# When the statistics of x1 are taken: a later place on VectorE, ScalarE and GpSimd in a two-layer graph kernel

## The chip, the cores and the metric

The kernel runs on one core of a Trainium2 chip. The metric is the device time of the whole program in microseconds: a median of 557.08 us over 3 runs (556.97 to 557.21). All data is float32 in HBM: a dense 4096 x 4096 adjacency matrix (67 MB) and node rows x of 4096 x 128.

## The reference, cut to what matters

```python
h = relu(layernorm(x))                       # first norm
x = x + gnn0(h, adj, weight, bias)           # x1: hyperbolic layer, support = adj @ x_tangent
h = relu(layernorm(x))                       # second norm: mean and variance of x1, row by row
x = x + gnn1(h, context, adj, ...)           # attention layer over the nonzeros of adj
```

Inside gnn0, after `support = adj @ x_tangent`, each row goes through expmap0, a projection, logmap0, a relu, expmap0 and a projection. All of these scale a row by a number made of its norm, so the kernel needs only sums of squares, powers, one tanh and a product. In gnn1 the logits are left[i] + right[j], and left and right are products of the 4096 x 256 context with two vectors.

## The kernel before, in words

**Phase 1** multiplies adj by x_tangent. It goes through 8 chunks c of 512 output rows. A chunk is 8 tiles of 1 MB, a tile 4 units, so a chunk has 32 units k. For each unit VectorE turns a block of adj (`turn_block`, L999) into one of four slots `turned`, TensorE multiplies it (L716, four matmuls), and ScalarE takes its signs for two units at once, a half (`signs`, L871, 16 halves a chunk), as the mask that phase 2 needs. VectorE may write unit k only when TensorE has done unit k - 4 and ScalarE has done the half with that unit. Tiles come by DMA into 6 slots, four at the end; two quarters of each are issued by SyncE, the other two by ScalarE after the odd halves (L299).

**The work behind a chunk.** The 512 rows p that chunk p has multiplied are finished while chunk p + 1 is being multiplied. Each engine has its steps at fixed places of its own loop:

- ScalarE: copy of the product after half 0, squares after half 4, tanh after half 9 of chunk p + 1; the normalised rows h2 (`normed`, L848, four activations) after half 2 of chunk p + 2.
- VectorE: relu after unit 7 (L1131), row sums after units 12 and 13 (L1135, L1139), then `spread` (L1145, bn_stats of x1) after units 28 and 29 and `variance` (L1152) after unit 30, all in chunk p + 1.
- GpSimd, in one list for p = 0 to 6: `shrink` (powers, L558 to L562), a piece of other work, `residual` (L569 to L573, which makes x1 in `xk`), `store_x1` (L589, four DMAs), a piece, `affine` (L579 to L582, scale and shift of the norm), a piece, `load_x` (L596, four DMAs that load the next x rows into `xk`).

The pieces are `beside(n)`: n even is a product of a part of context with a vector (L492), n odd the sums of such a product by halving (L501, 8 additions), for n = 0 to 15; n = 16 is `sums_and_rows` (L505 to L507), then `store_rows`, `widen_largest` and `exponents`. Pieces 0 to 7 run before p = 0, and piece 8 + 3p + j follows in p.

The waits that tie them together: `residual` waits for the tanh and for the x rows loaded; `spread` waits for `x1_ready`; `affine` waits for `var_ready`; `normed` waits for `norm2_ready` from `affine`; `load_x(p + 1)` waits for `h2_ready` from `normed`, because `normed` reads the same `xk`; `shrink(p + 1)` waits for `sums_ready`; relu(p + 1) waits for `x1_ready` of p.

**Phase 2** codes edges on VectorE and ScalarE from the mask and multiplies them by the weighted h2 rows on TensorE (L749).

Of the kernel before, what the change touches and what calls it, by code (L numbers as in the profile page):

```python
# [58 lines left out]
BESIDE_FIRST = 8  # L59
# [27 lines left out]
def bass_two_graph_layers(nc, x, adj, weight, bias, context, w_common, w_left, b_left, w_right, b_right, out):  # L87
# [3 lines left out]
    NC = N // CH  # L91
# [4 lines left out]
    with ExitStack() as ctx:  # L96
# [60 lines left out]
        def halves_of(dt, shape):  # L157

            n = L * CH
            return ([view(room, at * slot_bytes + half * n, shape, dt) for at in range(SLOTS)] for half in (0, 1))  # L160
        signs_of, _ = halves_of(I8, [L, CH])
# [279 lines left out]
        def _(pool):  # L441
# [46 lines left out]
            def product_of(w, part):  # L488

                ks = slice(part * BESIDE, (part + 1) * BESIDE)  # L490
                room_of = first_products if part == last_part else products
                side(tt(room_of, cx[:, ks, :], v_rows[:, w, :].unsqueeze(1).broadcast_to([P, BESIDE, C]), ALU.mult))  # L492

            def sum_of(w, part):

                ks = slice(part * BESIDE, (part + 1) * BESIDE)
                room_of = first_products if part == last_part else products
                n = C // 2
                while n:
                    dst = room_of[:, :, 0:n] if n > 1 else lr[:, w, ks].unsqueeze(2)  # L500
                    side(tt(dst, room_of[:, :, 0:n], room_of[:, :, n:2 * n], ALU.add))  # L501
                    n //= 2

            def sums_and_rows():
                tt(r_col[:], lr[:, 1, :], wlr[:, 3:4].broadcast_to([P, NK]), ALU.add).then_inc(r_ready, 1)  # L505
                side(tt(lr[:, 0, :], lr[:, 0, :], wlr[:, 2:3].broadcast_to([P, NK]), ALU.add))
                tt(neg_l, constants[:, 2:3].broadcast_to([P, NK]), lr[:, 0, :], ALU.subtract).then_inc(neg_ready, 1)  # L507
# [31 lines left out]
            def beside(n):  # L539

                w, part = turns[n // 2] if n < 2 * len(turns) else (None, None)
                if part is not None:
                    product_of(w, part) if n % 2 == 0 else sum_of(w, part)
                elif n == 2 * len(turns):
                    sums_and_rows()
                elif n == 2 * len(turns) + 1:
                    store_rows()
                elif n == 2 * len(turns) + 2:
                    widen_largest()
                elif n == 2 * len(turns) + 3:  # L550
                    exponents()
# [23 lines left out]
            def affine(p):  # L575

                pool.wait_ge(var_ready, p + 1)
                chain = Steps(pool, post_step, p * POOL_POST + 7)
                nc.gpsimd.tensor_scalar(post[:, 44:48], mv[:, :, 0], -1.0, None, ALU.mult)  # L579
                chain(nc.gpsimd.tensor_scalar(post[:, 40:44], mv[:, :, 1], LN_EPS, None, ALU.add))  # L580
                chain(tt(post[:, 48:52], post[:, 40:44], powers[:, 0:L], ALU.pow))
                tt(post[:, 36:40], post[:, 44:48], post[:, 48:52], ALU.mult).then_inc(norm2_ready, 1)  # L582
# [22 lines left out]
            for p in range(NC - 1):  # L605
                shrink(p)
                beside(BESIDE_FIRST + 3 * p + 0)
                if p == NC - 2:
                    scaled_weights()
                residual(p)  # L610
                store_x1(p)
                beside(BESIDE_FIRST + 3 * p + 1)
                affine(p)
                beside(BESIDE_FIRST + 3 * p + 2)
                load_x(p + 1)

            pool.wait_ge(weight_cols, 1)
# [142 lines left out]
        def _(act):  # L760
# [94 lines left out]
            def signs(c, parity):  # L855
                number = isinstance(c, int)
                acc_of[0] = acc[1 - parity]
                steps = {}
                if c >= 1:
                    copy, squares, tanh, _ = post_steps(c - 1)  # L860
                    steps = {0: copy, 4: squares, 9: tanh}
                if c >= 2:
                    steps[2] = post_steps(c - 2)[3]
                if c == NC - 2:
                    steps[7] = exponentials
                mc = mask[:, c].rearrange("p (s l) (h i) -> p l h s i", l=L, h=2)
                for half in range(TH):
                    act.wait_ge(block_turned, c * NK + HB * (half + 1))
                    slots = half % HALVES * HB
                    (l, h), s = run_and_half(c, half // HALVES), half % HALVES * L  # L870
                    nc.scalar.activation(mc[:, l, h, s:s + L],  # L871
                                         turned[:, slots:slots + HB, :].rearrange("p s (j i) -> p (s j) i", j=2),
                                         ACT.Sign, bias=constants[:, 4:5], scale=EDGE_SCALE).then_inc(
                        half_signed, 1)
                    if number and c == 0:
                        for n in range(XT_AHEAD + half * HB, min(NK, XT_AHEAD + (half + 1) * HB)):
                            bias_part(n)
                    if half in steps:
                        steps[half]()
                    if half % HALVES == HALVES - 1:  # L880
                        tile = behind[c * NC + half // HALVES]
                        if tile is not None:
                            load_tile(act, tile // NC, tile % NC, HIGH)
# [63 lines left out]
        def _(dve):  # L947
# [175 lines left out]
            def post_steps(p):  # L1123
                first = isinstance(p, int) and p == 0
                chain = Steps(dve, dve_step, p * POST + step.n)

                def relu():
                    dve.wait_ge(support_turned, p + 1)
                    if not first:
                        dve.wait_ge(x1_ready, p)  # L1130
                    v.tensor_scalar(relu_u[:], support, 0.0, None, ALU.max).then_inc(relu_ready, 1)  # L1131

                def sums_u():
                    dve.wait_ge(u_squared, p + 1)
                    v.reduce_sum(post[:, 0:4], sq1, AX_X)  # L1135

                def sums_relu():
                    dve.wait_ge(relu_squared, p + 1)
                    v.reduce_sum(post[:, 4:8], sq2, AX_X).then_inc(sums_ready, 1)  # L1139

                def spread(ls):
                    if ls[0] == 0:
                        dve.wait_ge(x1_ready, p + 1)
                    for l in ls:
                        ins = v.bn_stats(stats[:, l, :], xk[:, l, :])  # L1145
                    if ls[-1] == L - 1:
                        chain(ins)

                def variance():
                    v.memset(post[:, 61:62], 0.0)  # L1150
                    for l in range(L):
                        ins = v.bn_aggr(mv[:, l, :], stats[:, l, :])  # L1152
                    ins.then_inc(var_ready, 1)
                return {7: relu, 12: sums_u, 13: sums_relu, 28: lambda: spread((0, 1)), 29: lambda: spread((2, 3)),
                        30: variance}


            def turn(c, parity):
                number = isinstance(c, int)
                steps = {} if number and c == 0 else post_steps(c - 1)  # L1160
                for k in range(NK):
                    if not (number and c == 0 and k < TSLOTS):
                        turn_block(c, k)
                    if number and c == 0 and k // L % 2 == 0:
                        for k_ in blocks_of(c, k):
                            tangent(tangent_order.index(k_))
                    if k in steps:
                        steps[k]()
                    if c == NC // 2 and k == 15:
                        dve.wait_ge(r_ready, 1)  # L1170
                        v.reduce_max(extreme[:, 0:1], r_col[:], AX_X).then_inc(top_ready, 1)
                        dve.wait_ge(neg_ready, 1)
                        v.transpose(neg_rows, neg_l).then_inc(neg_turned, 1)
                    if c == NC // 2 + 1 and k == 3:
                        dve.wait_ge(top_spread, 1)
                        v.reduce_max(extreme[:, 1:2], ps_top, AX_X).then_inc(top_ready, 1)
            for c in range(NC):
                turn(c, c % 2)
            last = [f for _, f in sorted(post_steps(NC - 1).items())]

            def compare(c, parity, g):
                slot_free(dve, c, g)
# [140 lines left out]
```

## Time and profile before

| | us |
|---|---|
| median of 3 runs | 557.08 |
| the profiled execution, whole | 554.63 |
| its span, first to last instruction | 552.8 |
| TensorE busy in it | 480.3 |
| VectorE busy | 447.1 |
| ScalarE busy | 314.0 |
| GpSimd busy | 271.7 |

All times in the rows and in the prediction are microseconds from the start of the span of that one execution. In a timeline, a line is: start, duration, engine, source line, operation, output and input, count of merged instructions, and in brackets the idle time ahead of it with the engine that ended it. The chain of waits is the path that ended last, followed back from the end.

### The profile page before, as it was taken

Reading aid. Unit: us, or ns where it says so; the run is one execution under the profiler, and the core shown is the slowest. Engines: PE = TensorE matmul, PEld = TensorE weight load, DVE = VectorE, ACT = ScalarE, POOL = GpSimd, SP = SyncE. Lnnn points to the kernel's source line nnn. Section 1 sums busy time; section 2 is a strip of 40 time slices with the busy share of each in tenths; the row PEclk is TensorE's granted clock in tenths of the full one; section 3 lists DMA queues with packets and bytes.
Section 4 is the critical chain, followed back from the end, with each engine's and each line's share of the span. In section 5 each row is a group of like instructions: output and inputs, shape, how many; then the busy total and the mean of one; then the engine's idle time right before and its main releaser. Section 6 shows DMA issues by size and latency. Waiting matters only on the chain.

```text
span 552.8 us, 9390 instructions
## 1 busy us (share of the span) xinstructions
PE 480.3 (87%) x3209; PEld 413.2 (75%) x3209; DVE 447.1 (81%) x907; ACT 314.0 (57%) x466; POOL 271.7 (49%) x348
## 2 busy tenths in 40 slices
PE   1733879999999999999994777899999999999995
PEld 1622758877787788888883556788888888888884
DVE  3997878777787798888888899968788787878763
ACT  1584767748586778686866632535353535353521
POOL 6840899999999675535357996202020202020200
PEclk9985999999999999999997879999999999999998
DMA  7899999999999999998970000110101010101010
GB/s 171 186 234 223 252 300 301 275 280 266 311 289 320 260 332 320 338 293 218 273 194 20 22 18 28 32 40 20 39 18 41 13 46 8 52 2 38 1 39 20
DMA packets 91851, 84.75 MB, mean 153 GB/s; under 512 B 7552, under 2 KB 89728, under 8 KB 91808
## 3 DMA queue, kind: packets, MB, share of 16 engines
q1 hardware_dynamic: 56032, 48.64, 35.4%
q10 hardware_dynamic: 33424, 31.20, 20.5%
q0 software_dynamic: 2352, 4.35, 2.9%
q8 instruction: 25, 0.41, 0.3%
q14 instruction: 18, 0.15, 0.1%
HBM read 79.96 MB, written 4.21 MB: 152 GB/s over the span
## 4 chain that ended last, share of the span: by engine, by line
PE 54%; POOL 24%; DVE 7%; SPq 7%; issue 3%; DMA 3%; ACT 2%; ACTq 0%; POOLq 0%; DVEq 0%
PE ps L749 35%; PE ps L716 19%; POOL mask L501 8%; POOL mask L492 7%; SPq L382 3%; SPq L299 2%; DVE room L1234 2%; DMA mask<-in_L_gnn_context_dram 2%; DVE room L1201 2%; SPq L373 2%; DVE room L1185 1%; POOL out_dram L589 1%; POOL post L559 1%; POOL xk L596 1%; DVE room L1208 1%
## 5 line engine op out<-in xcount | busy, mean ns | idle before, releaser
L716 PE MATMUL ps<-room 128*128 128x256 f32 x1024 | 227.9, 382 | 28.5 <-DVE room L1117 22.7
L749 PE MATMUL ps<-room 128*128 128x258 f16 x2048 | 232.3, 276 | 20.5 <-POOL room L629 15.0
L749 PEld LDWEIGHTS ps<-room 128*128 128x128 fp8e4 x2048 | 200.5, 98 | 52.3 <-issue 16.0
L716 PEld LDWEIGHTS ps<-room 128*128 128x128 f32 x1024 | 193.4, 191 | 60.6 <-DVE room L999 27.5
L871 ACT ACTIVATE mask<-room,constants 128x1024 int8<-128x1024 f32 x128 | 146.1, 1145 | 59.0 <-DVE room L999 56.3
L999 DVE STREAM_TRANSPOSE room<-room 128x512 f32<-128x512 f32 x184 | 124.5, 697 | 19.8 <-PE ps L716 11.2
L643 POOL TENSOR_TENSOR h_room<-h_room 128x512 f32<-128x512 f32 x7 | 8.9, 1275 | 146.3 <-DVE post L1275 146.3
L1201 DVE SCALAR_TENSOR_TENSOR room<-mask,constants,room 128x512 int32<-128x512 int32 x64 | 64.5, 1007 | 10.8 <-ACT room L919 10.8
L919 ACT ACTIVATE room<-relu_u,r_col 128x512 int8<-128x512 f32 x64 | 42.0, 713 | 40.6 <-PE ps L749 40.6
L919 ACT ACTIVATE room<-room,r_col 128x512 int8<-128x512 f32 x62 | 40.9, 712 | 34.5 <-PE ps L749 34.5
L999 DVE STREAM_TRANSPOSE room<-mask 128x512 f32<-128x512 f32 x72 | 48.9, 697 | 8.6 <-PE ps L716 4.2
L1208 DVE SCALAR_TENSOR_TENSOR room<-mask,constants,room 128x512 int32<-128x512 int32 x64 | 48.3, 754 | 0.3
L492 POOL TENSOR_TENSOR mask<-mask,h_room 128x2048 f32<-128x2048 f32 x8 | 36.4, 4544 | 22.9 <-DMA mask<-in_L_gnn_context_dram 22.5
L501 POOL TENSOR_TENSOR mask<-mask 128x1024 f32<-128x1024 f32 (+6 forms) x56 | 45.0, 804 | 4.2
L1185 DVE TENSOR_SCALAR room<-room,r_col 128x512 int8<-128x512 f32 x66 | 36.6, 598 | 9.3 <-PE ps L749 9.3
L940 ACT ACTIVATE h_room<-ps,factors 128x258 f32<-128x258 f32 x32 | 15.2, 477 | 48.7 <-PE ps L749 47.7
L1185 DVE TENSOR_SCALAR room<-relu_u,r_col 128x512 int8<-128x512 f32 x64 | 32.1, 542 | 9.9 <-PE ps L749 9.9
L1264 DVE SCALAR_TENSOR_TENSOR h_room<-ps,factors,h_room 128x258 f32<-128x258 f32 x32 | 15.2, 484 | 16.8 <-ACT h_room L940 16.1
L596 POOL DMA_DIRECT2D xk<-in_x_dram x32 | 18.1, 571 | 20.5 <-ACT h_room L848 19.9
L848 ACT ACTIVATE h_room<-xk,post 128x128 f32<-128x128 f32 x32 | 13.1, 481 | 16.0 <-POOL post L582 16.0
L589 POOL DMA_DIRECT2D out_dram<-xk x32 | 18.3, 582 | 2.4 <-POOL xk L573 2.4
L1234 DVE SCALAR_TENSOR_TENSOR room<-h_room,factors,room 128x128 f16<-128x128 f32 x32 | 16.7, 581 | 0.0
(160 smaller groups left out, 343.1 us busy)
## 6 DMA issues: line engine op xcount, KB each, us to landing
room<-in_adj_dram SPq DMA_DIRECT2D x100, 256.0 KB, 7.6
room<-in_adj_dram ACTq DMA_DIRECT2D x84, 256.0 KB, 8.3
mask<-in_adj_dram SPq DMA_DIRECT2D x40, 256.0 KB, 8.1
mask<-in_adj_dram ACTq DMA_DIRECT2D x32, 256.0 KB, 9.0
mask<-in_L_gnn_context_dram SPq DMA_DIRECT2D x16, 256.0 KB, 11.7
xk<-in_x_dram POOLq DMA_DIRECT2D x32, 64.0 KB, 6.4
out_dram<-xk POOLq DMA_DIRECT2D x32, 64.0 KB, 4.8
h_room<-out_dram SPq DMA_DIRECT2D x32, 64.0 KB, 2.4
```

The source lines that it names most:

```text
L492: side(tt(room_of, cx[:, ks, :], v_rows[:, w, :].unsqueeze(1).broadcast_to([P, BESIDE, C]), ALU.mult))
L501: side(tt(dst, room_of[:, :, 0:n], room_of[:, :, n:2 * n], ALU.add))
L589: pool.dma_start(out_n[p, b], xk[b * Q:(b + 1) * Q]).then_inc(x1_stored, 16)
L716: mm = pe.matmul(acc[parity][:, h], xt[:, tangent_order.index(blocks_of(c, k)[j]), :], turned[:, k % TSLOTS, j * (CH // 2):(j + 1) * (CH / ...
L749: mm = pe.matmul(ps[:, 2 * t + w, 0:GW], part[slot(c, g)][:, kk, t * P:(t + 1) * P], G[w][:, k, :], start=(k == 0), stop=(k == NK - 1))
L871: nc.scalar.activation(mc[:, l, h, s:s + L], turned[:, slots:slots + HB, :].rearrange("p s (j i) -> p (s j) i", j=2), ACT.Sign, bias=const ...
L919: ins = nc.scalar.activation(signs_of[slot(c, g)][:, kk, :], nl[parity], ACT.Sign, scale=-1.0, bias=r_col[:, k:k + 1])
L999: v.transpose(turned[:, k % TSLOTS, :].rearrange("p (j r i) -> p j r i", j=2, r=RH), loaded[slot_of[c * NC + g]][:, :, 2 * l * Q:2 * (l + ...
L1185: ins = v.tensor_scalar(signs_of[slot(c, g)][:, kk, :], nl[parity], r_col[:, k:k + 1], -1.0, ALU.is_gt, ALU.mult)
L1201: v.scalar_tensor_tensor(out=neg_words[n], in0=edges_of(c, g), scalar=ones, in1=neg_words[n], op0=ALU.bitwise_and, op1=ALU.bitwise_and).th ...
L1208: v.scalar_tensor_tensor(out=pos_words[n], in0=edges_of(c, g), scalar=ones, in1=neg_words[n], op0=ALU.bitwise_and, op1=ALU.bitwise_xor).th ...
L1234: v.scalar_tensor_tensor(out=G[1][:, k, D:2 * D], in0=h2[:, k, :], scalar=s1_col[:, k:k + 1], in1=G[1][:, k, 0:D], op0=ALU.mult, op1=ALU.s ...
```

## The change

Three places move; no operation is added or taken away.

- VectorE takes `spread` and `variance` of rows p after units 3, 4 and 5 of chunk p + 2, no longer after units 28 to 30 of chunk p + 1. The rows p = 6 keep their place, units 28 to 30 of the last chunk.
- ScalarE makes `normed` after half 5 of chunk p + 2, no longer after half 2.
- GpSimd does both later pieces of p between `store_x1` and `affine`; before, the second came between `affine` and `load_x`.

```diff
                 residual(p)
                 store_x1(p)
                 beside(BESIDE_FIRST + 3 * p + 1)
+                beside(BESIDE_FIRST + 3 * p + 2)
                 affine(p)
-                beside(BESIDE_FIRST + 3 * p + 2)
                 load_x(p + 1)
...
                 if c >= 2:
-                    steps[2] = post_steps(c - 2)[3]
+                    steps[5] = post_steps(c - 2)[3]
...
-                return {7: relu, 12: sums_u, 13: sums_relu, 28: lambda: spread((0, 1)), 29: lambda: spread((2, 3)),
-                        30: variance}
+                return [relu, sums_u, sums_relu], [lambda: spread((0, 1)), lambda: spread((2, 3)), variance]
...
-                steps = {} if number and c == 0 else post_steps(c - 1)
+                steps = {}
+                if c >= 1:
+                    steps.update(zip((7, 12, 13), post_steps(c - 1)[0]))
+                if c >= 2:
+                    steps.update(zip((3, 4, 5), post_steps(c - 2)[1]))
+                if c == NC - 1:
+                    steps.update(zip((28, 29, 30), post_steps(c - 1)[1]))
```

## Rows read from the trace of the kernel before

**Rows 1.** The page's span in 40 slices of 13.8 us, busy tenths
```profile
POOL 6840899999999675535357996202020202020200
PEclk9985999999999999999997879999999999999998
```
**Rows 2.** The chain of waits: start, us, what; from ScalarE's norm to chunk 7
```profile
184.49 0.33 ACT h_room L848
...
188.05 20.24 PE ps L716 x92
...
238.30 0.44 PE ps L703 x4
238.74 27.63 PE ps L716 x128
```
**Rows 3.** VectorE's timeline: relu of chunks 1, 5 and 7; spread at unit 28
```profile
91.55 0.65 DVE L1131 TENSOR_SCALAR relu_u<-ps 128x512 f32<-128x512 f32 x1
...
112.63 0.49 DVE L1145 BATCH_NORM_STATS2 stats<-xk 128x6 f32<-128x128 f32 x2 [2.62 <-POOL xk L573]
...
212.21 0.65 DVE L1131 TENSOR_SCALAR relu_u<-ps 128x512 f32<-128x512 f32 x1
...
268.34 0.65 DVE L1131 TENSOR_SCALAR relu_u<-ps 128x512 f32<-128x512 f32 x1
...
286.53 0.45 DVE L1145 BATCH_NORM_STATS2 stats<-xk 128x6 f32<-128x128 f32 x2
```
**Rows 4.** GpSimd's timeline around affine and load_x, p = 0, 1, 2
```profile
121.69 0.22 POOL L579 TENSOR_SCALAR post<-mv 128x4 f32<-128x4 f32 x1
...
123.57 4.53 POOL L492 TENSOR_TENSOR mask<-mask,h_room 128x2048 f32<-128x2048 f32 x1
128.40 2.26 POOL L596 DMA_DIRECT2D xk<-in_x_dram  x4 [0.29 <-POOL mask L492]
...
151.17 0.22 POOL L579 TENSOR_SCALAR post<-mv 128x4 f32<-128x4 f32 x1
...
153.04 6.09 POOL L501 TENSOR_TENSOR mask<-mask 128x1024 f32<-128x1024 f32 x7
...
184.26 0.20 POOL L582 TENSOR_TENSOR post<-post 128x4 f32<-128x4 f32 x1
...
186.73 2.25 POOL L596 DMA_DIRECT2D xk<-in_x_dram  x4 [1.57 <-ACT h_room L848]
```
**Rows 5.** ScalarE's timeline: norm of rows 2, and the signs after it
```profile
184.49 0.49 ACT L848 ACTIVATE h_room<-xk,post 128x128 f32<-128x128 f32 x1 [2.96 <-POOL post L582]
...
186.04 2.17 ACT L871 ACTIVATE mask<-room,constants 128x1024 int8<-128x1024 f32 x2
```
**Rows 6.** TensorE's timeline: idle gaps ahead of matmuls, in brackets
```profile
113.78 5.74 PE L716 MATMUL ps<-room 128*128 128x256 f32 x24 [1.32 <-DVE room L999]
...
300.31 5.00 PE L749 MATMUL ps<-room 128*128 128x258 f16 x32 [7.12 <-POOL room L629]
...
312.40 5.35 PE L749 MATMUL ps<-room 128*128 128x258 f16 x32 [2.98 <-POOL room L629]
321.79 9.70 PE L749 MATMUL ps<-room 128*128 128x258 f16 x64 [4.04 <-POOL room L629]
...
352.01 8.21 PE L749 MATMUL ps<-room 128*128 128x258 f16 x73 [2.25 <-DVE room L1208]
```
**Rows 7.** Stretches: each engine's busy us, then granted TensorE clock (PEclk), DMA share, GB/s
```profile
299.80:303.30 3.50, 2.99 (x16) 2.15 (x17) 3.50 (x4) 1.19 (x2) 3.36 (x4) 0.54 0.00 0
...
313.50:316.90 3.40, 3.40 (x18) 2.42 (x17) 3.40 (x7) 2.53 (x7) 3.03 (x4) 0.53 0.07 19
...
323.70:327.20 3.50, 3.50 (x19) 2.51 (x18) 3.50 (x7) 0.00 (x0) 3.12 (x5) 0.54 0.00 0
```
**Rows 8.** DMAs: issue to landing of L299's tiles, and of the x rows
```profile
DMA to landing us min/median/max: 4.8/8.0/16.7
...
DMA to landing us min/median/max: 2.1/6.4/7.9
```

More of the change, by code:

```diff
@@ L1178, in _ @@
                 turn(c, c % 2)
-            last = [f for _, f in sorted(post_steps(NC - 1).items())]
+            last = [f for part in post_steps(NC - 1) for f in part]
             def compare(c, parity, g):
```

## The prediction, made before the changed kernel was built

> **What bounds the kernel now.** I read the page's slices first, then the chain of waits, then the timelines of the four engines through phase 1. The slices show GpSimd full from about 57 to 180 us and half empty afterwards, and the granted clock at its full level through the whole of phase 1 [rows 1]. The chain of waits runs on GpSimd up to 184.5 us, passes through ScalarE's norm, the signs behind it and one turned unit on VectorE, and from 188.05 stays on TensorE until phase 1 ends at 292 [rows 2]. So the first half of phase 1 goes at the pace of GpSimd's list, and the second half at TensorE's.
>
> TensorE's own pace is 27.63 us for 128 matmuls and 0.44 for four transposes: 28.07 a chunk, 0.863 a unit [rows 2]. I mark each chunk by its relu, right after VectorE's unit 7. From chunk 1 (91.55) to chunk 5 (212.21) four chunks take 120.66 us, where TensorE alone would take 112.3: 8.4 us are lost there. From chunk 5 to chunk 7 (268.34) two chunks take 56.13 us, exactly the pace [rows 3]. A change that moves only where stalls fall can therefore gain at most 8.4 us.
>
> In chunks 1 to 3 what binds is x1: VectorE waits 2.4 to 2.6 us for it at unit 28, three times, of which the first stands [rows 3]. In chunk 4 it is the norm at half 2: ScalarE waits 2.96 us for affine, takes the norm, and only then makes the signs that free VectorE's slots [rows 5].
>
> **The change part by part.**
>
> Spread and variance, VectorE. The 12 instructions cost the same time. The x1 of rows p may now come 7 units later plus the slot lead that unit 28 used up; all three waits of this kind disappear: x1 of rows 0 stood ready at 112.6 [rows 3], and even if GpSimd's list falls 4 us behind, as below, x1 of rows 2 comes at 177.4, before unit 3 of chunk 4. In units 3 to 7 VectorE gets some 1.3 us more beside TensorE; it has up to four units in hand, and unit 7 waits for TensorE today. I take 0.
>
> Norm at half 5, ScalarE. Three halves later is 6 units, 5.2 us of allowance. It now comes right behind the squares of half 4 (1.1 us). Signs of half 6 come about 1 us late, and VectorE has more lead than that. I take 0. Queued behind the wait for affine are the signs of half 6 and ScalarE's two DMAs for a tile, weighed below.
>
> The two pieces ahead of affine, GpSimd. Here the cost lies. In the list of p = 0 the second piece is a product (4.53 us), in p = 1 it is a sum (6.09 us for seven additions, about 6.4 with the eighth), in p = 2 three small additions: 0.7 us, what GpSimd was busy in the 2.27 us up to load_x, of which it was idle 1.57 [rows 4]. Affine comes later by just that. And `load_x(p + 1)` now stands right behind affine and waits for the norm. With nothing between them, L582 ends at 184.46 and the DMAs start at 186.73: 2.27 us. Behind a piece of work the same start takes 0.29 [rows 4]. So GpSimd, which in this stage has no idle time, gets 1.97 us of it in each p.
>
> Now I follow GpSimd's list. It is unchanged until affine of p = 0 would begin, 121.69 [rows 4].
> - p = 0: product first, affine begins at 126.3 and ends at 128.2 (1.9 from 121.69 to the product's start at 123.57). Norm starts at 128.27. The x rows are issued until 132.75 instead of 130.66: the list is 2.1 late.
> - p = 1: affine began at 151.17; now 2.1 for the late list and 6.4 for the sum come ahead of it, so it begins at 159.65 and ends at 161.57. Norm starts at 161.6.
> - p = 2: the list is 2.1 + 2.0 = 4.1 late; affine ended at 184.46, now 184.46 + 4.1 + 0.7 = 189.3.
>
> From a late norm to TensorE: today norm starts at 184.49 [rows 5] and TensorE resumes with unit 10 at 188.05, so 3.56 us [rows 2]. From half 5 it resumes with unit 16. From there to the next chunk's relu are 20 units (17.27), the transposes (0.44) and 0.69, the turn of VectorE's unit 7, which starts when TensorE has done unit 3 and ends in the relu: 18.40. The same sum for today's half 2 gives 211.7 where 212.21 was observed, 0.5 too early; part of that is VectorE's sums at units 12 and 13, which no longer follow the restart, so I add 0.2 to the later results.
> - Chunk 3's relu: 128.27 + 3.56 + 18.40 = 150.2 (today 152.78).
> - Chunk 4's relu: 161.6 + 3.56 + 18.40 + 0.2 = 183.8 (today 182.29).
> - Chunk 5's relu: by its own norm 189.3 + 21.96 = 211.3; by TensorE's pace 183.8 + 28.07 = 211.8. The later holds, 211.8, against 212.21.
>
> So the waits for x1 and the wait in chunk 4 go, and one long wait in chunk 3 takes nearly all of it: **a gain of 0.4 us** and no more, if the clock holds.
>
> It probably does not. TensorE would have run ahead to the end of unit 15 of chunk 3: unit 16 would be due 9.7 us after the relu of 150.2 (12 units from the end of unit 3, less the turn of unit 7), at 159.95, and starts at 161.6 + 3.56 = 165.2. **TensorE is idle for 5.2 us**. Today TensorE's largest gap from chunk 1 to 7 is 1.32, and the clock stays full [rows 1, 6]. In phase 2 the granted clock falls from the full level, 2.4 GHz, to the lower of its two levels, 1.2 GHz, around the gaps of 7.12, 2.98 and 4.04 us, and not around one of 2.25 [rows 6, 7]. TensorE then worked at the lower level from 300.31 to 303.3, from 313.5 to 316.9 and from 321.79 to 327.2: 3.0, 3.4 and 5.4 us, in which half the work gets done [rows 6, 7]. The price is 1.5, 1.7 or 2.7, mean **2.0 us**. After the restart VectorE turns a unit in 0.65 to 0.70, faster than TensorE takes one at either level, so that price lies wholly on the path. In chunk 2 the gap would be 131.8 - 129.3 = 2.5 us; a fall there costs nothing, since chunk 3 waits anyway.
>
> The Trainium skill, "TensorE: Matmul & The Clock Gate", Part 1, says that the throttled clock is the default and activity releases it, so that an idle engine drops back. By that rule the gap in chunk 3 costs something at its restart; without it the sum ends at the 0.4 us of gain. The three gaps here agree.
>
> **The sum.** Relu of chunk 5: 211.8 + 2.0 = 213.8 against 212.21, 1.6 us later. From there TensorE's pace and phase 2 are unchanged: the rows of p = 6 keep their place. I apply the difference to the median, 557.08; the profiled execution (554.63, span 552.8) lies 2.4 below that. **Forecast 558.6 us**, with 557.9 to 559.6 as its own range (clock price 1.5 to 2.7, and 0.2 to 0.3 for the restart).
>
> **The rivals.**
> 1. The clock holds in chunk 3. Everything else as above: -0.4 us, 556.7. It decides on the gap: with 2.3 us or less the rows show no fall, with 3.0 and more three out of three. It would need affine(1) 2 us or more earlier, or TensorE that much less far ahead. Chance 0.2. This is also the case that is not slower.
> 2. The stalls really go. The allowance, 7 units for x1 and 5.2 us for the norm, exceeds every wait of today (2.62 for x1, 2.96 for the norm [rows 3, 5]). If GpSimd lost nothing by its new order, affine(1) delayed by the sum alone would put relu 5 at 209.8 or less; if the list kept up fully, the whole 8.4 us would return. That gives 548.7 to 555. Against it: GpSimd is full until 184 [rows 1], and the wait of load_x is in the program. Chance 0.12.
> 3. A DMA becomes late. ScalarE's two quarters for the tile freed at half 5 of chunk 3 are issued at 161.6 instead of at 155.5, and the tile is due as unit 0 of chunk 4, about 175.5. That leaves 13.9 us; the landing takes 8.0 at the median, 16.7 at most [rows 8]. Price up to 2.8. In the same way the x rows of p = 6, issued from about 7.4 to 9.7 us after the relu, land at 15.5 (17 at the most), x1 is ready at 17 and is asked for at 18.2 [rows 3, 8]: price up to 0.5. With the clock's price the end is 559.5 to 561.5. Chance 0.1.
> 4. The reorder leaves the order of events as it is, and the sum of small shifts stays within 1 us. Chance 0.03.
>
> **How the numbers follow.** The forecast has the remaining 0.55. About 0.2% (1.1 us) is what a measurement of this kernel can tell from no change. Of the forecast's 0.55, 0.1 falls within that. Slower: 0.45 + 0.1 = 0.55. Same: 0.1 + 0.2 + 0.03, and faster 0.12. The range for 8 in 10 leaves out most of rival 2 and the far end of rival 3: 556.3 to 560.3.
>
> **What the profile would show.** Right: no wait at VectorE's spread; GpSimd idle 2 us ahead of load_x in p = 0, 1, 2; ScalarE waiting for affine at half 5 of chunk 3 for about 6 us, and about 3 in chunk 2; affine(1) ending near 161.6; TensorE idle for about 5 us near 160 to 165 and a granted clock below 1 there; relu of chunk 4 near 185.8 and of chunk 5 near 213.8; 28.07 a chunk from there. Wrong: a full clock in that stretch (rival 1), relu of chunk 5 before 211 (rival 2), a VectorE wait for a tile in chunk 4 (rival 3). The weakest step is the clock's price, which depends on when within the gap the level changes; the next is the 0.2 us for the restart.

## The result and the profile after

The changed kernel takes 558.18 us (median of 20 runs) against 555.61 us for the kernel before, measured in turn with it (20 runs): a ratio of 1.0040, 95% interval 1.0024 to 1.0057. It is slower by 0.4%. In a second series (12 runs against 28) the ratio was 1.0034 (1.0019 to 1.0049). The profiled execution has a span of 557.9 us, 5.1 more than that of before; a second profile of the same kernel has 555.5. The forecast, 558.6, was made from a base of 557.08, so it meant +1.6. Measured are +2.6 between the medians of the first series and +1.1 between those of the second; by the ratios it is +2.2 and +1.9.

The page after, slices, against [rows 1]:

```profile
POOL 6840899997979683717177996202020202020200
PEclk9985999999988999999996979899999999999998
```

GpSimd has holes where it was full, and the granted clock has a dip in phase 1, slices 12 and 13. TensorE's timeline of chunks 2 to 5 (start, duration, matmuls, idle ahead; L999 is VectorE's turn of a unit, L703 the transposes):

```profile
118.58 11.39 PE L716 MATMUL ps<-room 128*128 128x256 f32 x52
132.31 16.67 PE L716 MATMUL ps<-room 128*128 128x256 f32 x76 [2.34 <-DVE room L999]
...
149.26 11.39 PE L716 MATMUL ps<-room 128*128 128x256 f32 x52
165.72 19.43 PE L716 MATMUL ps<-room 128*128 128x256 f32 x76 [5.07 <-DVE room L999]
184.98 0.60 PE L703 MATMUL ps<-ident,room 128*128 128x128 f32 x4
185.42 26.07 PE L716 MATMUL ps<-room 128*128 128x256 f32 x120
```

Two gaps of the chunks are left where before had five of 0.9 to 1.3, both ahead of unit 16 (52 matmuls are 13 units from unit 3 on). The same 76 matmuls take 16.67 us after the first gap and 19.43 after the second. What ended the gaps stands in ScalarE's timeline:

```profile
128.73 0.49 ACT L848 ACTIVATE h_room<-xk,post 128x128 f32<-128x128 f32 x1 [3.33 <-POOL post L582]
...
162.13 0.49 ACT L848 ACTIVATE h_room<-xk,post 128x128 f32<-128x128 f32 x1 [6.06 <-POOL post L582]
```

The norm (L848) waits for affine (it ends in L582), 3.3 and 6.1 us, against 2.96 at the most before [rows 5]. And GpSimd's timeline, against [rows 4]:

```profile
122.13 4.54 POOL L492 TENSOR_TENSOR mask<-mask,h_room 128x2048 f32<-128x2048 f32 x1
126.76 0.22 POOL L579 TENSOR_SCALAR post<-mv 128x4 f32<-128x4 f32 x1
...
128.49 0.20 POOL L582 TENSOR_TENSOR post<-post 128x4 f32<-128x4 f32 x1
130.97 2.26 POOL L596 DMA_DIRECT2D xk<-in_x_dram  x4 [2.28 <-ACT h_room L848]
...
153.72 6.08 POOL L501 TENSOR_TENSOR mask<-mask 128x1024 f32<-128x1024 f32 x7
159.88 0.20 POOL L501 TENSOR_TENSOR h_room<-mask 128x8 f32<-128x8 f32 x1
160.18 0.22 POOL L579 TENSOR_SCALAR post<-mv 128x4 f32<-128x4 f32 x1
...
161.89 0.20 POOL L582 TENSOR_TENSOR post<-post 128x4 f32<-128x4 f32 x1
164.37 2.25 POOL L596 DMA_DIRECT2D xk<-in_x_dram  x4 [2.28 <-ACT h_room L848]
```

The sum stands ahead of affine, affine of rows 1 ends at 162.1 (before 153.1), and load_x idles for 2.28 us instead of 0.3. For rows 2 it idles for 4.51 us (3.46 in the second profile), where the prediction had about 2; by then TensorE sets the pace. VectorE's wait for x1 is gone in all chunks. The relus against [rows 3]:

| relu of chunk | before | after | after, second profile | forecast |
|---|---|---|---|---|
| 1 | 91.55 | 92.22 | 91.65 | 91.55 |
| 2 | 121.49 | 120.28 | 119.71 | 119.6 |
| 3 | 152.78 | 150.96 | 152.86 | 150.2 |
| 4 | 182.29 | 187.12 | 186.38 | 185.8 |
| 5 | 212.21 | 215.41 | 214.67 | 213.8 |
| 7 | 268.34 | 271.54 | 270.80 | 269.9 |
| relu 7 to the end | 284.49 | 286.40 | 284.72 | 284.5 |

(Relu 2 of the forecast is relu 1 plus the pace; 185.8 is 183.8 plus the clock's 2.0.) So 2.5 to 3.2 us are lost by relu 5, in chunk 3, and the first profile shows 1.9 more behind relu 7, the second 0.2. The 1.7 us between these two come from one place in phase 2. TensorE restarts there behind a gap of 2.25 us in every profile of this case, of both kernels. The timeline (its last matmuls cut off by the window) and the 4 us behind the restart (busy us of TensorE, weight loads, VectorE, ScalarE, GpSimd, then the granted clock), the first profile and then the second:

```profile
355.45 4.81 PE L749 MATMUL ps<-room 128*128 128x258 f16 x27 [2.25 <-DVE room L1213]
...
355.45:359.45 4.00, 4.00 (x22) 2.92 (x23) 4.00 (x6) 0.29 (x1) 1.37 (x1) 0.57 0.24 49
```
```profile
354.70 5.57 PE L749 MATMUL ps<-room 128*128 128x258 f16 x49 [2.25 <-DVE room L1213]
...
354.70:358.70 4.00, 4.00 (x37) 3.52 (x38) 4.00 (x6) 0.55 (x2) 1.37 (x1) 1.00 0.23 49
```

Behind the same gap the clock fell in the first and held in the second. From this restart to the end are 202.5 us in the first profile and 200.8 in the second, as in both profiles of the kernel before. From relu 7 to this restart the changed kernel takes 83.9 us and the kernel before 83.7, in both profiles of each: 0.2 us that belong to the change.

### The profile page after: what moved, and what is told of

Same layout as the page of the kernel before. It is cut to its first block, busy times and chain, and to the rows that moved or that the text cites. A ratio compares the mean times of both kernels' runs of the same rounds, so it can differ in the third digit from the quotient of the medians.

```text
span 557.9 us, 9395 instructions
## 1 busy us (share of the span) xinstructions
PE 480.6 (86%) x3209; PEld 415.5 (74%) x3209; DVE 451.3 (81%) x907; ACT 314.3 (56%) x466; POOL 272.1 (49%) x348
## 4 chain that ended last, share of the span: by engine, by line
PE 63%; DVE 16%; POOL 11%; ACT 4%; issue 3%; ACTq 1%; DMA 1%; POOLq 0%; DVEq 0%
PE ps L749 35%; PE ps L716 27%; POOL mask L501 3%; POOL mask L492 2%; DVE room L1239 2%; DVE room L1206 2%; ACT mask L871 2%; DVE room L999 2%; DVE room L1190 1%; DVE mask L957 1%; DVE room L1213 1%; DVE mask L1011 1%; POOL out_dram L589 1%; DVE mask L1007 1%; DMA mask<-in_x_dram 1%
## 5 line engine op out<-in xcount | busy, mean ns | idle before, releaser
L716 PEld LDWEIGHTS ps<-room 128*128 128x128 f32 x1024 | 196.7, 194 | 60.5 <-DVE room L999 25.9
L999 DVE STREAM_TRANSPOSE room<-room 128x512 f32<-128x512 f32 x184 | 126.5, 701 | 22.3 <-PE ps L716 12.2
L999 DVE STREAM_TRANSPOSE room<-mask 128x512 f32<-128x512 f32 x72 | 49.0, 698 | 15.9 <-ACT mask L871 8.9
L848 ACT ACTIVATE h_room<-xk,post 128x128 f32<-128x128 f32 x32 | 13.1, 481 | 20.5 <-POOL post L582 20.5
L1239 DVE SCALAR_TENSOR_TENSOR room<-h_room,factors,room 128x128 f16<-128x128 f32 x32 | 18.4, 634 | 0.0
```

The lines of the kernel that those rows point to most:

```text
L716: mm = pe.matmul(acc[parity][:, h], xt[:, tangent_order.index(blocks_of(c, k)[j]), :], turned[:, k % TSLOTS, j * (CH // 2):(j + 1) * (CH / ...
L999: v.transpose(turned[:, k % TSLOTS, :].rearrange("p (j r i) -> p j r i", j=2, r=RH), loaded[slot_of[c * NC + g]][:, :, 2 * l * Q:2 * (l + ...
L1239: v.scalar_tensor_tensor(out=G[1][:, k, D:2 * D], in0=h2[:, k, :], scalar=s1_col[:, k:k + 1], in1=G[1][:, k, 0:D], op0=ALU.mult, op1=ALU.s ...
```

## The experiments

GpSimd's list starts between 101.0 and 102.3 us in every profile and sets the pace, so relu 5 is best counted from the start of the span. The expectations count from relu 1; that serves where relu 1 comes at 91 to 93 us, and flatters e1 and e8, where it came at 94.9 and 94.7. "Time" is the median of the series; ratios are to the kernel before in the same series.

### The changed kernel once more

> The changed kernel as it is, for a second profile beside the experiments. Theory (GpSimd's list makes the norm of rows 1 late, TensorE is idle for 5 us in chunk 3 and its clock falls): from the relu of chunk 1 to the relu of chunk 5 122.5 to 124 us as in the first profile (before: 120.7), 1.0 to 3 us over the kernel before; the time at the lower clock level after the gap may differ from profile to profile. Rival (the difference comes from phase 2, where the first profile shows 1.9 us more from relu 7 to the end): phase 1 at 120.7 in another profile.

Time 557.43 us, ratio 1.0034 (1.0019 to 1.0049). Relu 1 to relu 5 is 123.02, as expected. In this execution the clock fell in chunk 2 as well: the 76 matmuls after that gap took 18.19 us, those in chunk 3 18.36. The fall in chunk 2 made the gap in chunk 3 shorter (3.50 us) and so cost nothing by itself. The loss of phase 1 is there in both profiles; that of phase 2 is not, so it can't be the main cause. So the rival of this expectation falls.

### One part undone: GpSimd's list

```diff
                 beside(BESIDE_FIRST + 3 * p + 1)
-                beside(BESIDE_FIRST + 3 * p + 2)
                 affine(p)
+                beside(BESIDE_FIRST + 3 * p + 2)
                 load_x(p + 1)
```

> The new places on VectorE and ScalarE, GpSimd's list in its old order (second piece between affine and load_x). Theory: GpSimd's list runs as before, affine of rows 1 ends near 153.1 and of rows 2 near 184.5; the waits for x1 at unit 28 are gone, chunks 2 and 3 go at 28.1 us, one gap of about 2.5 us of TensorE is left in chunk 4. Relu 1 to relu 5: 115.1 us, or up to 116.8 if the clock falls at that gap, so 4 to 5.6 us faster than the kernel before and about 7 to 8 faster than the changed one. Rival (VectorE and ScalarE are crowded at units 3 to 7 and halves 4 to 5, or ScalarE's tile DMAs are late behind the wait): still slower than or equal to the kernel before, chunks above 28.5 us.

Time 553.64 us, ratio 0.9946 (0.9928 to 0.9964). Relu 5 comes at 209.53, 2.7 to 3.2 us before that of the kernel before (relu 1 to relu 5 is 114.6). With the old list the same places on VectorE and ScalarE make the kernel 0.5% faster than before instead of 0.3 to 0.4% slower, with chunks 1 and 2 at 28.06 and 28.07 us: the units 3 to 7 and the neighbourhood of squares and norm crowd nobody. But only 3 us came, not 4 to 5.6, and the gap left was not the one that I named:

```profile
166.57 0.20 ACT L839 ACTIVATE post<-post 128x4 f32<-128x4 f32 x1 [3.92 <-POOL post L561]
...
169.50 9.76 PE L716 MATMUL ps<-room 128*128 128x256 f32 x44 [1.86 <-DVE room L999]
```

(ScalarE's, then TensorE's timeline.) ScalarE waited 3.9 us for shrink, for the tanh after half 9 of chunk 3; TensorE stood before unit 24. I had left this wait out. In this profile the clock had also fallen before relu 1, ahead of anything that the change touches. That may hold part of the missing gain: GpSimd's list starts 0.9 us later than in the first profile of the kernel before and waits 1.28 us for the norm ahead of load_x of rows 1, not 0.29.

### Only the sum goes back behind affine

```diff
                 beside(BESIDE_FIRST + 3 * p + 1)
-                beside(BESIDE_FIRST + 3 * p + 2)
+                if p != 1:
+                    beside(BESIDE_FIRST + 3 * p + 2)
                 affine(p)
+                if p == 1:
+                    beside(BESIDE_FIRST + 3 * p + 2)
```

> The changed kernel, but in p = 1 alone the sum goes back between affine and load_x. Theory: affine of rows 1 ends near 155.2, no long gap in chunk 3; the list is still about 2 us late from load_x's wait in p = 0, and affine of rows 2 ends at 187.3. Relu 1 to relu 5: 118.0 us (up to 119.7 with a fall of the clock in chunk 4), 1 to 2.7 us faster than the kernel before. If instead the wait of load_x were the main cost, it would stay within 1 us of the changed kernel, 122 to 123.

Time 554.68 us, ratio 0.9978 (0.9963 to 0.9993); relu 1 to relu 5 is 118.65. The second is as expected (118.0, up to 119.7). Relu 5 comes at 210.31: this one piece of 6.4 us in one p makes up 4.4 to 5.1 of the 5.1 to 5.9 us between the changed kernel (214.67 and 215.41) and e1 (209.53), and 2.8 of the 3.8 us between their medians. The rest, under 1 us by relu 5, is left for the product ahead of affine in p = 0 and load_x's wait.

### Filling the gap of chunk 3

The added matmuls write to a bank that nothing reads. With them the gap holds work, so that the clock can be told from the lateness of the norm.

```diff
+                    if k == 15 and c == 3:
+                        for _ in range(20):
+                            pe.matmul(ps[:, 4, 0:2 * P], ident[:], xt[:, 0:2, :].rearrange("p a d -> p (a d)"),
+                                      start=True, stop=True)
```

> The changed kernel with 20 more matmuls of 128x256 on TensorE after unit 15 of chunk 3, into a bank that nothing reads: 4.3 us of work inside the gap of 5.1 us. Nothing else changes. Theory: the clock stays at its full level in chunk 3, TensorE restarts at the same time, and relu 1 to relu 5 is 120.3 to 120.7 us instead of 123.2: 2 to 3 us less than the changed kernel, about level with the kernel before. Rival (the clock is not what makes the rest of chunk 3 slow; late tiles or crowding are): the granted clock still falls or chunk 3 stays as long, time as the changed kernel or up to 4 us worse.

Time 562.09 us, ratio 1.0107 (1.0080 to 1.0133), worse by 4 to 5 us than the changed kernel. The filler was mis-sized: the trace shows 40 matmuls, 8.8 us, for 20 calls, and TensorE went on with unit 16 at 170.09 instead of 165.7. The clock itself did what was expected, the 76 matmuls after it took 16.57 us, but the time decides nothing. So once more with 8 calls:

> As e4_filler with 8 calls in place of 20. The profile of e4_filler shows two recorded matmuls of 0.216 us to a call, so its 20 calls filled 8.6 us and put off the restart; 8 calls are 3.5 us, shorter than the gap. Theory (the clock's fall): the filler ends before unit 16 is due, the granted clock stays full in chunk 3, the 76 matmuls after the gap take 16.6 to 16.8 us instead of 18.4 to 19.4, and relu 1 to relu 5 is 120.3 to 121.5 us against 123.0 to 123.2 of the changed kernel: 1.5 to 2.9 us less. Rival (what is slow after the gap isn't the clock): relu 1 to relu 5 stays at 123.

Time 556.89 us, ratio 1.0019 (1.0004 to 1.0034). TensorE's timeline:

```profile
149.39 11.39 PE L716 MATMUL ps<-room 128*128 128x256 f32 x52
160.62 3.62 PE L723 MATMUL ps<-room,ident 128*128 128x256 f32 x16
165.80 16.67 PE L716 MATMUL ps<-room 128*128 128x256 f32 x76 [1.57 <-DVE room L1003]
```

The restart is at the same time as in the changed kernel (165.80 against 165.72), and the 76 matmuls behind it take 16.67 us, not 19.43. The stretch just after the restart, in the changed kernel and then with the filler (busy us of TensorE, its weight loads, VectorE, ScalarE, GpSimd, then the granted clock):

```profile
166.40:170.00 3.60, 3.60 (x10) 2.88 (x9) 2.22 (x4) 2.39 (x3) 3.27 (x6) 0.50 1.10 211
```
```profile
166.40:170.00 3.60, 3.60 (x18) 3.18 (x17) 3.47 (x6) 2.48 (x3) 3.27 (x6) 1.00 1.12 217
```

At the lower level, 1.2 GHz, 10 matmuls; at the full one 18, with the same work on GpSimd and more on VectorE. Relu 5 comes at 212.74, 1.9 to 2.7 us earlier than in the two profiles of the changed kernel, and level with the kernel before (212.21 and 212.70). Relu 1 to relu 5 (118.1) says too much, since in this profile relu 1 was late at 94.7. The times don't separate the two: the ratios to the kernel before (1.0019 and 1.0034, from two series) differ by 0.8 us in the filler's favour with intervals that overlap, and the distances of the medians, 1.6 and 1.1 us, point the other way. So the price of the clock is shown in one trace against three (two of the changed kernel and that of e10), and not by the times.

### Each part alone

GpSimd's part alone, on the kernel before:

```diff
                 beside(BESIDE_FIRST + 3 * p + 1)
+                beside(BESIDE_FIRST + 3 * p + 2)
                 affine(p)
-                beside(BESIDE_FIRST + 3 * p + 2)
```

> The kernel before with GpSimd's part of the change alone: both pieces ahead of affine; spread stays at units 28 to 30, norm at half 2. Theory: affine of rows 1 ends near 161.6 and of rows 2 near 189.3, and the norm at half 2 has 5.2 us less allowance than in the changed kernel. Relu 1 to relu 5: 126 us, up to 129 with falls of the clock, so 5.3 to 8 us slower than the kernel before and 3 to 5.5 slower than the changed one. Rival (the order of the list is harmless, VectorE's new units are what costs): within 1 us of the kernel before.

Time 566.43 us, ratio 1.0188 (1.0163 to 1.0213). Relu 1 to relu 5 is 130.9, beyond the 129 expected; the gaps are 4.33 and 5.41 us, and the clock fell in chunks 1, 2 and 3. The list is what costs, and the later places of the norm and of the statistics soften it; which of the two does is not separated.

VectorE's part alone (spread and variance a chunk later; norm at half 2 and the list as before):

```diff
-                    steps[5] = post_steps(c - 2)[3]
+                    steps[2] = post_steps(c - 2)[3]
```

> VectorE's part of the change alone: spread and variance after units 3 to 5 a chunk later; norm at half 2 and GpSimd's list as before. Theory: the three waits for x1 (7.6 us in all) go, but the norm at half 2 then meets the same affine: it ends at 184.5 for rows 2 as before, so relu 5 comes at the same time. Relu 1 to relu 5: 120.7 us, time within 1 us of the kernel before. Rival (waits that go are time gained): 113 to 115.

Time 558.18 us, ratio 1.0056 (1.0036 to 1.0076). The waits for x1 are gone, and nothing is gained: ScalarE's norm now waits 4.5 and 4.4 us for affine of rows 0 and 2, where it had waited 2.9 and 3.0. Relu 1 to relu 5 is 122.2, 1.5 more than expected, behind two gaps ahead of unit 10 of 3.05 and 2.87 us, and the clock fell after the first:

```profile
127.70 24.83 PE L716 MATMUL ps<-room 128*128 128x256 f32 x100 [3.05 <-DVE room L999]
...
190.09 20.24 PE L716 MATMUL ps<-room 128*128 128x256 f32 x92 [2.87 <-DVE room L999]
```

A chain that runs on GpSimd only lets one wait be exchanged for another. The time is 3 us above the kernel before, where I had expected it within 1 us. In this profile VectorE also waits 3.5 us for the last tiles of chunk 7, and phase 2's restart comes 85.2 us after relu 7, 1.5 later than before; why the tiles were late is open. The clock fell behind the restart, which makes up another 1.6.

ScalarE's part alone (norm at half 5):

```diff
-                    steps[2] = post_steps(c - 2)[3]
+                    steps[5] = post_steps(c - 2)[3]
```

> ScalarE's part of the change alone: norm after half 5, spread at units 28 to 30 and GpSimd's list as before. Theory: the waits for x1 at unit 28 still set chunks 1 to 3 (relu 4 at 182.3), and only chunk 4's wait for affine goes. Relu 5 at 210.5 us (before 212.2): about 1.6 us faster than the kernel before. Rival (the squares and the norm next to each other crowd ScalarE): equal or slower.

Time 556.0 us, ratio 1.0006 (0.9985 to 1.0028), a median level with the kernel before. Relu 5 is at 210.9 as expected (210.5), the span 551.6, but the expected 1.6 us don't show in the times. The profiled execution was the fastest of ten, from 553.4 to 560.4; this one is inconclusive.

### A version that beats both

```diff
-                    steps = {0: copy, 4: squares, 9: tanh}
+                    steps = {0: copy, 4: squares, (12 if c in (2, 3, 4) else 9): tanh}
                 if c >= 2:
-                    steps[5] = post_steps(c - 2)[3]
+                    steps[7 if c == 4 else 5] = post_steps(c - 2)[3]
```

with GpSimd's list in its old order.

> e1_old_list (the new places of VectorE and ScalarE, GpSimd's list in its old order), and ScalarE takes two steps later where GpSimd's list is late: tanh after half 12 instead of 9 in chunks 2, 3 and 4, the norm of rows 2 after half 7 instead of 5 in chunk 4. Theory: the wait for tanh of 3.9 us in chunk 3 of e1_old_list goes and the norm of chunk 4, ready at 184.5, comes when it is asked for; TensorE has no gap from chunk 1 to 7. Relu 1 to relu 5: 112.5 to 113 us (before 120.7, e1 114.6), about 8 us faster than the kernel before, 1.6 to 2 us faster than e1. Rival (VectorE and ScalarE are too crowded for 28.1 us a chunk while GpSimd is full): 114 or more.

Time 550.7 us, ratio 0.9911 (0.9889 to 0.9932): 0.9% faster than the kernel before. Relu 5 is at 205.89, 6.3 to 6.8 us before that of the kernel before. Relu 1 to relu 5 is 114.6 rather than 112.5 to 113, in the range that I had given to the rival. Still TensorE runs chunks 1, 2 and 3 at its own pace (28.1 us from transposes to transposes), which the rival denies; what is left lies in chunk 4, where x1 of rows 2 is now 1.9 us late for VectorE's unit 3 and the gap ahead of unit 16 is 0.48. So some 2 us of the 8 remained. With the norm of chunk 4 back at half 5:

> e7_tanh_norm with the norm back at half 5 in chunk 4: the new places of VectorE and ScalarE, GpSimd's old list, tanh after half 12 in chunks 2 to 4. Theory: no gap in chunk 3; in chunk 4 the norm waits for affine of rows 2 (184.5) and TensorE resumes with unit 16 at 188.1. Relu 5 at 206.8 us, 1 us behind e7_tanh_norm (205.9), which showed that the last wall there is worth only that. Rival (the tanh's place makes no difference): a gap of 2 us ahead of unit 24 of chunk 3, relu 5 at 207.5 or later.

Time 551.71 us, ratio 0.9925 (0.9898 to 0.9952). Relu 5 is at 206.92, and ScalarE's wait ends as worked out:

```profile
184.46 0.49 ACT L848 ACTIVATE h_room<-xk,post 128x128 f32<-128x128 f32 x1 [2.29 <-POOL post L582]
...
188.05 14.94 PE L716 MATMUL ps<-room 128*128 128x256 f32 x68 [1.67 <-DVE room L999]
```

The gap ahead of unit 24 in chunk 3 is gone, so the tanh was that wall. The two versions can't be told apart by their times.

### The end of phase 1

> The changed kernel without the load of the x rows for p = 6 (four DMAs of 64 KB in chunk 7): x1 of those 512 rows is then made from what lies in the tile, so this part of the computation is left out. In profiles of the changed kernel VectorE waits 1.1 to 1.8 us for the last tiles of adj in chunk 7, where the kernel before shows no such wait, and the x rows are now issued at 7.3 us after the relu instead of 1.2 us, together with the last tiles. Theory A (the x rows delay the last tiles): the wait goes, relu 7 to the end is 1 to 2 us shorter than the changed kernel's 284.7 to 286.4, and the time 1 us less. Theory B (the last tiles are only just in time whatever the x rows do): the wait stays between 0.5 and 2.5 us.

This version leaves out the load of the x rows of p = 6, and its x1 of these rows is made from what lies in the tile.

```diff
-                pool.wait_ge(xk_loaded, p * (16 * NQ) + 16 * NQ)
+                pool.wait_ge(xk_loaded, (p - (p >= NC - 2)) * (16 * NQ) + 16 * NQ)
...
+                if p == NC - 2:
+                    return
                 for b in range(NQ):
```

In chunk 7 the first profile of the changed kernel shows a wait that the first profile of before does not, on VectorE at unit 28:

```profile
289.99 0.71 DVE L999 STREAM_TRANSPOSE room<-room 128x512 f32<-128x512 f32 x1 [1.10 <-DMA room<-in_adj_dram]
```

Without the x rows, issued in the changed kernel 7.3 us after the relu (278.80) instead of 1.2 (269.58), this wait is gone, and relu 7 to the last relu is 25.58 us as in the kernel before, against 26.49 and 26.61 in the changed one. But nothing was gained by it: the time is 557.66 us, ratio 1.0032 (1.0014 to 1.0050), relu 7 to the end is 286.8, and phase 2's restart comes 84.4 us after relu 7, later than the changed kernel's 83.9. Nor do the waits of the other profiles go by the x rows: e5, which issues them 2.9 us after the relu, waits 3.5 us for the last tiles, and e1 and e6, which issue them at 7.3, wait 0.5 and 0.6. So that the x rows hold up the last tiles is not shown, and what the wait costs on the path is nothing here.

> The kernel before, for a second profile. Relu 5 at 212.2 us again, since GpSimd's list sets it. If a wait of 0.5 us or more for the last tiles shows here too, and relu 7 to the end is 286 instead of 284.5, these belong to both kernels; if it is again 284.5 without a wait, the change costs there as well.

Time 555.09 us, ratio 0.9986 (0.9969 to 1.0004) to the shared runs. Relu 5 at 212.7, relu 7 to the end 284.5. Here too VectorE waits for the last tiles, twice and shorter:

```profile
283.17 2.14 DVE L999 STREAM_TRANSPOSE room<-room 128x512 f32<-128x512 f32 x3 [0.45 <-DMA room<-in_adj_dram]
286.60 0.71 DVE L999 STREAM_TRANSPOSE room<-room 128x512 f32<-128x512 f32 x1 [0.43 <-DMA room<-in_adj_dram]
```

So part of that wait belongs to both kernels. Behind relu 7 the profiles fall into two groups by the restart at phase 2's gap of 2.25 us. In five of the fourteen the clock held there (both of the kernel before, the second of the changed one, e6 and e9), and from the restart to the end are 200.8 us in each. In the other nine it fell, and there are 202.4 to 202.5. That is 1.6 to 1.7 us by which a profile, and so a single run, can be longer than another of the same kernel. Whether the changed kernel meets this fall more often than the kernel before, one of two profiles against none of two can't tell.

## Why the prediction was right, point by point

- **Direction and size.** Forecast +1.6 us, measured +2.6 in the first series (1.3 to 3.2 by the ratio's interval). 558.18 lies inside 556.3 to 560.3, and inside the likeliest case's own 557.9 to 559.6. That the absolute time was met to 0.4 us is in part luck: the base taken from three runs, 557.08, was 1.5 above the median of twenty, and the difference was 1.0 too small.
- **VectorE at no cost.** Right in phase 1's chunks: no wait for x1, chunk 1 at 28.06 us after, chunks 1 and 2 in e1 too. Not traced to an engine are the 0.2 us more between relu 7 and phase 2's restart, which the prediction put at nothing: 83.9 us or more in all profiles with VectorE's new places, 83.7 in all four without.
- **The sum ahead of affine, and load_x's wait.** Right in place and size: affine(1) ended at 162.1 for 161.6 forecast, load_x's idle was 2.28 us for 2.27. 0.45 of the 0.5 us is a later start of the list (101.70 for 101.25). e1 and e2 show the list as the cause, and e3 the sum as its main part.
- **ScalarE at half 5 at no cost.** Right for squares and norm. But I had not carried the third step that hangs on GpSimd's list, the tanh after half 9. In the changed kernel it is hidden behind the longer wait (0.7 us); in e1 it was the wall and made my expectation too good, by 1.2 us to judge by the ratios of e9 and e1 and by 2.6 to judge by their relu 5. The term was missing from the replay, and it would have been found by asking for each step of ScalarE what it waits for.
- **Chunk 5 by TensorE's pace.** Right, with 28.29 for that chunk instead of 28.07: two matmuls of `ps_top` (L725) come between. A term of 0.22 left out; it is also part of the 0.5 us by which the prediction's sum missed today's 212.21, and which it put down in part to VectorE's sums.
- **The clock.** The step on which the sign hung. The gap was 5.07 us (forecast 5.2), the clock fell, and the price was 19.43 - 16.67 = 2.8 us where 2.0 stood, and 1.7 in the other profile. The filler shows that it is the clock. With the clock held, relu 5 is at 212.74 and not at 211.8, so the case without a fall would have been about level and not a gain of 0.4: of the 0.9 us between, 0.6 came from the later restart (165.80 for 165.2) and 0.2 from L725.
- **The restart.** 165.72 + 17.27 + 0.44 + 0.69 + 2.8 gives 186.9 for relu 4, observed 187.12; the 0.2 that I had added is borne out.
- **Rival 1** (the clock holds) did not occur in the three profiles with this gap unfilled (two of the changed kernel and e10). **Rival 2** fell as argued: it needs the old list, and then gives what e1, e9 and e7 show. **Rival 3** did not occur where it was placed: no tile was late in chunk 4, and x1 of rows 6 was in time. Tiles were late in chunk 7 (1.10 us), for a cause that is open, and e10 shows no price for it.
- **Phase 2 unchanged.** Right but for the 0.2 us above and the clock at the gap of 2.25 us. The prediction took that gap as one at which the clock holds, by the one profile that it had; it fell there in nine of fourteen.

## What to carry to other kernels

When a chain of waits runs on one full engine, a consumer that asks later gains only if the producer does not also deliver later: move the consumer's place, and keep everything that others wait for ahead of the engine's free work. Independent work put between a result and a wait on its consumer (here the piece between affine and load_x) hides that wait, and moving it ahead pays twice. Follow every step that reads from that engine, since the next one a little behind the first becomes the wall: here x1, norm, tanh and then x1 again, within 2 us of each other. And before a difference between two profiles is put down to a change, compare the granted clock behind the gaps that both have: one fall at a gap of the same length made 1.7 us here.

## What the runs showed of the hardware

- The clock can fall after a shorter gap than the rows before had shown. In the second profile of the kernel before it fell behind one of 1.64 us, and the same 24 matmuls that take 5.74 us elsewhere took 7.38:

```profile
114.36 7.38 PE L716 MATMUL ps<-room 128*128 128x256 f32 x24 [1.64 <-DVE room L999]
```

  It also fell behind 1.89 (e2, chunk 1), 2.10 (e4, chunk 2) and 2.95 us (e3, chunk 2), while it held behind 2.34 (the changed kernel, above), 2.87 (e5, chunk 4) and even 3.00 us in the profile of ScalarE's part alone:

```profile
145.14 5.74 PE L716 MATMUL ps<-room 128*128 128x256 f32 x24 [3.00 <-DVE room L999]
```

  The cleanest case is phase 2's gap of 2.25 us, the same in all fourteen profiles: the clock held behind it in five and fell in nine. So one and the same kernel differs from execution to execution, and with it the price of its gaps. The bound of my rival 1 (no fall with 2.3 us or less, a fall with 3.0 or more) held on neither side. Behind every gap in chunks 1 to 7 longer than 3.00 us, from 3.05 to 5.41, the clock fell.
- A matmul call of 128x256 in float32 is recorded as two matmuls: 8 calls gave 16 records in 3.62 us (e8), 20 calls 40 in 8.80 (e4). At the full clock a record takes 0.216 us of a busy stream (27.63 us for 128 [rows 2]).
- Behind a gap filled with matmuls the clock held: with 16 records in the 5.1 us ahead of unit 16 (e8) the 76 matmuls behind took 16.67 us, with 40 (e4) 16.57, and 18.36 to 19.60 in the three profiles with the gap empty.
